# Output squares of a gated delta-rule layer: summed by ScalarE's accumulator, tile by tile, instead of through a buffer and a VectorE sum

## The reference

```
_, out = jax.lax.scan(step, S0, xs)            # the heads' outputs, 128 features each
xn = _rms_norm(out) * norm_w                   # out * rsqrt(mean(out^2) + eps)
gated = jax.nn.silu(z) * xn
return gated.reshape(b_, s_, VALUE_DIM) @ W_out
...
x = _layernorm(x + attention(x));  x = _layernorm(x + experts(x))
```

## Time and profile before

| | |
|---|---|
| median of 3 runs | 1535.07 us (1533.1 to 1536.61) |
| profiled execution | 1533.56 us, its span 1531.8 us |
| PE / PEld busy | 1450.4 us (95%) / 1170.5 us (76%) |
| DVE busy | 1137.3 us (74%) |
| ACT busy | 1067.1 us (70%) |
| POOL busy | 705.5 us (46%) |
| squares L776 | 64 instructions of 128x512, mean 632 ns |
| sums L978 | 64 instructions, mean 677 ns |
| squares of the keys L679 | 128 ACTIVATE of 128x128, mean 293 ns, and 128 accumulator reads, mean 225 ns |

### The profile page before, as it was taken

One profiled execution on the slowest core, in us unless ns is written; L12 is line 12 of the kernel. 1 busy time (PEld: TensorE's weight loads), 2 busy tenths in 40 slices (PEclk: granted clock), 3 DMA queues, 4 the chain that ended last, 5 costly groups with the idle time before them and its releaser, 6 DMA issues.

```text
span 1531.8 us, 38664 instructions
## 1 busy us (share of the span) xinstructions
PE 1450.4 (95%) x14988; PEld 1170.5 (76%) x14988; DVE 1137.3 (74%) x1982; ACT 1067.1 (70%) x2136; POOL 705.5 (46%) x619
## 2 busy tenths in 40 slices
PE   5689999999999999999999999999978899999996
PEld 3468889898888989898888989888864556656565
DVE  5579999999999998999999898999855432312314
ACT  6577878878787787878778777878655365464640
POOL 0544544545454544555454545545316354353540
PEclk9899999999999999999999999999999899999998
DMA  3000202112020311202021120202231112002100
GB/s 113 1 1 23 57 6 53 30 30 36 23 57 2 57 23 36 36 23 56 2 56 20 39 36 23 46 13 43 36 87 51 35 35 69 34 34 69 34 0 28
DMA packets 100985, 55.70 MB, mean 36 GB/s; under 512 B 74572, under 2 KB 93016, under 8 KB 100824
## 3 DMA queue, kind: packets, MB, share of 16 engines
q1 hardware_dynamic: 100824, 53.47, 14.2%
HBM read 35.62 MB, written 1.05 MB: 24 GB/s over the span
## 4 chain that ended last, share of the span: by engine, by line
PE 72%; issue 12%; POOL 8%; DVE 4%; ACT 2%; DMA 1%; POOLq 0%; SPq 0%; DVEq 0%; ACTq 0%
PE bank L387 11%; POOL h L1623 7%; PE bank L542 6%; PE bank L588 5%; PE bank L485 5%; PE bank L529 5%; PE bank L577 4%; PE bank L559 4%; PE bank L568 3%; PE bank L477 3%; PE bank L469 3%; PE bank L1321 3%; PE bank L437 2%; PE bank L438 2%; PE bank L413 2%
## 5 line engine op out<-in xcount | busy, mean ns | idle before, releaser
L874 DVE SCALAR_TENSOR_TENSOR con<-bank,taps,con 128x1022 f32<-128x1022 f32 (+2 forms) x192 | 245.2, 1277 | 13.1 <-ACT con L657 8.6
L1623 POOL TENSOR_TENSOR h<-h 128x512 f16<-128x512 f32 x120 | 148.1, 1242 | 172.4 <-ACT h L1412 166.6
L1516 DVE SCALAR_TENSOR_TENSOR facc<-bank,gcol,facc 128x256 f32<-128x256 f32 x96 | 42.0, 479 | 220.2 <-PE bank L1321 220.2
L1030 POOL TENSOR_TENSOR gl<-const_sb,gc 128x512 f16<-128x512 f32 x128 | 129.7, 1041 | 152.7 <-DVE gc L884 83.0
L387 PE MATMUL bank<-x,qkv 128*128 128x512 f16 x768 | 182.6, 389 | 10.2 <-DVE con L874 10.1
L1305 PE MATMUL bank<-y,w 128*128 128x512 f16 x720 | 166.6, 381 | 8.0 <-ACT h L1412 5.5
L1411 ACT ACTIVATE h<-bank,b 128x512 f32<-128x512 f32 x120 | 82.4, 687 | 127.2 <-PE bank L1305 125.0
L1321 PE MATMUL bank<-w,h 128*128 128x256 f16 x1440 | 160.8, 274 | 0.0
L1321 PEld LDWEIGHTS bank<-w,h 128*128 128x128 f16 x1440 | 141.6, 98 | 19.9 <-issue 0.7
L932 DVE TENSOR_TENSOR X<-X,bank 128x512 f16<-128x512 f16 x192 | 130.0, 683 | 30.7 <-PE bank L477 29.2
L726 ACT ACTIVATE Z<-bank 128x512 f16<-128x512 f16 x192 | 114.2, 606 | 46.2 <-PE bank L485 44.6
(11 more groups left out here) (211 smaller groups left out, 3885.0 us busy)
## 6 DMA issues: line engine op xcount, KB each, us to landing
w<-in_w SPq DMA_DIRECT2D x24, 640.0 KB, 4.5
w_qkv<-in_W_qkvz SPq DMA_DIRECT2D x16, 512.0 KB, 4.1
w_z<-in_W_qkvz SPq DMA_DIRECT2D x16, 256.0 KB, 2.8
w_out<-in_W_out SPq DMA_DIRECT2D x16, 256.0 KB, 3.0
Z<-in_xT SPq DMA_DIRECT2D x2, 512.0 KB, 5.0
y<-in_x SPq DMA_DIRECT2D x1, 1024.0 KB, 8.1
sqo<-oo SPq DMA_TRANSPOSE x64, 3.1
out_dram<-y SPq DMA_DIRECT2D x8, 128.0 KB, 1.8
```

The source lines that it names most:

```text
L874: stt(out=out, in0=bank[:, 0:B, 0:S - k], scalar=taps[:, par, t, TAPS - 1 - k:TAPS - k], in1=out, op0=ALU.mult, op1=ALU.add).then_inc(tap_ ...
L1030: last = tt(gl[:, g % 2, k].rearrange("p (m r) d -> p m r d", m=2), upper.unsqueeze(1).unsqueeze(1).broadcast_to([P, 2, R, P]), gc[:, par, ...
L1623: tt(h16[:, par, 1, t, at], h32[:, k % H32], h16[:, par, 0, t, at], ALU.subtract)\
```

## The change

Squares go to ScalarE's accumulator. For each of the 4 tiles of a chunk, one ACTIVATE (Square, 128x128) with `accum_out` writes the sum of the tile's squares straight to its column of `sso`. The squares themselves are still written, to a place where nobody reads them: the tile's place in the high half of `oo16` (fp16), which "high" overwrites later. The VectorE sums go; its eps step stays and now waits for the fourth square step of its head. `sqo` goes, and `oT` gets memory of its own. The waits change with it: squares now wait for the head before's power (which reads `sso`) and transposes (which read `oo16`), and the transposes of groups 0 and 1 for "op" 2 and 3 of the head before instead of the sums. `sum_done` counts 1 per head instead of 5.

```
+    oT = sb("oT", [P, 2, 2, 4, P], F16)
-    sqo = sb("sqo", [P, 2, B, R, P])
-    oT = sqo[:].rearrange("p s b r d -> p s (b r d)").bitcast(F16).rearrange("p s (k u d) -> p s k u d", k=2, u=4)
...
             sp.wait_ge(oo_low, 4 * n + g + 1)
-            if g < 2:
-                sp.wait_ge(sum_done, 5 * n + 5)
-            else:
-                is_full(sp, n, ("op", g - 2))
+            is_full(sp, n, ("op", g - 2) if g >= 2 else ("op", g + 2, 1))
...
         def square_out(n, par, c):
             is_free(act, n, ("pdl", c))
-            if after(n, 1) or c >= 2:
-                act.wait_ge(sum_done, 5 * n + c - 1)
-            if c < 2:
-                is_full(act, n, ("op", 2 + c, 1))
-            last = do(sqo[:, c % 2], oo[:].rearrange("p (b c r) d -> p b c r d", b=B, c=CH)[:, :, c], ACT.Square)
+            if c == 0 and after(n, 1):
+                act.wait_ge(rso_ready, n + 1)
+            if after(n, 1):
+                act.wait_ge(oT_in[c // 2], 16 * n)
+                act.wait_ge(oT_in[2 + c // 2], 16 * n)
+            for b in range(B):
+                for r in range(R):
+                    u = (b * CH + c) * R + r
+                    last = do(oo16[:, u // 4, 0, u % 4], oo[:, u], ACT.Square, accum_out=sso[:, u:u + 1])
             last.then_inc(sq_out, 1)
...
         def sum_squares(n, par, c):
-            if c == 0 and after(n, 1):
-                dve.wait_ge(rso_ready, n + 1)
-            dve.wait_ge(sq_out, CH * n + c + 1)
-            nc.vector.tensor_reduce(sso[:].rearrange("p (b c r) -> p b c r", b=B, c=CH)[:, :, c], sqo[:, c % 2],
-                                    AX, ALU.add).then_inc(sum_done, 1)
             if c == CH - 1:
-                dve.wait_ge(sum_done, 5 * n + CH)
+                dve.wait_ge(sq_out, CH * n + CH)
...
-            pool.wait_ge(sum_done, 5 * n + 5)
+            pool.wait_ge(sum_done, n + 1)
```

## The result

| | before | changed |
|---|---|---|
| median, lowest to highest | 1535.26 us (1533.1 to 1536.61, 8 runs) | 1539.95 us (1539.13 to 1542.05, 8 runs) |
| profiled execution, span | 1533.56, 1531.8 us | 1539.23, 1537.2 us |
| DVE busy | 1137.3 us | 1100.2 us |
| ACT busy | 1067.1 us | 1103.5 us |

The recorded ratio is 1.0026 with a 95% interval from 1.0017 to 1.0035: slower by 4.0 us (2.6 to 5.4), where the two medians of the table lie 4.7 us apart. The kernel is slower by more than nothing. A second series of the changed kernel gave 1.0027 (1.0015 to 1.0038).

The account below looks back on a forecast made before the run. The prediction took TensorE, idle 0.12 us per head, as full. Waits of 3.15 us plus 0.64 in the last head gave 3.8 us: 1537.4 for the profiled execution, median 1538.9 (+0.25%), range 1534.8 to 1544.

Parts of the forecast that it names:

- The price of a tile: ScalarE's squares: distance between starts of two squared tiles, accumulator read included, 0.29 us; bounds 0.25 and 0.48.
- The row that reads PSUM: Keys' squares, same instruction reading PSUM, 0.25 us per tile; basis of the cheap-tile rival, no new wait, 1535.55, chance 0.30.
- The place: Chunks 2 and 3 on ScalarE: delays add before the "turn" copy, TensorE's L477 waits 0.21 us per head.
- The count of the waits: TensorE's wait behind the "turn" copy, in heads 0 to 14: 15 x 0.21 = 3.15 us.
- Chunks 0 and 1 at nothing: Squares of chunks 0 and 1 on ScalarE: L477 has 0.9 us of slack, cost 0 up to t = 0.40.
- Taps "just in time": VectorE's taps: the copies they need are through at 625.2, and the taps start at 625.24.
- VectorE's relief at nothing: VectorE's four removed sums per head, about 40 us over 16 heads, set nothing earlier for TensorE; costed at 0.
- Last head 0.64: Last head: ScalarE's L1223 behind chunk 3's squares starts 0.64 us later, delaying VectorE's L1233 and L994; cost 0.64 us.
- The signs that the prediction named: Profile after: L477 waits 0.1 to 0.3 us for ACT 15 times, heads last 67.8 us, L1233 waits 0.6 us longer.
- TensorE's reserve: Rival: weight loads busy 58.57 of 67.60 us, so TensorE catches up; only 0.64 us stays, 1535.7, chance 0.08.
- the prices 1562.5 and 1542.6: Times for dearer tiles: 1562.5 at t = 0.48 (dear-tile rival, chance 0.07), 1542.6 at t = 0.32.
- the 1537.4: Forecast for the profiled execution: 3.8 us added to its 1533.56; for a median, 1538.9.

Follow-up runs that it names:

- the kernel without accumulator: Changed kernel with its four narrow squares per chunk but no accumulator output, sums left out; 1537.95 us in one execution.
- the fifth tile: Changed kernel plus a fifth squared tile with accumulator behind chunk 3's four, its result unread; 1544.65 us, ratio 1.0057.
- the sums gone: Kernel before with VectorE's four sums per head left out and nothing in their place, squares 512 columns wide; 1535.97 us, ratio 1.0003.
- the sums put back: Changed kernel with VectorE's four reductions per head back at their old places, over a constant into a spare place; 1541.08 us, ratio 1.0034.
- one exchange in the queue: Changed kernel with ScalarE's turn of level 2, half 1 ahead of chunk 3's squares instead of behind; 1536.46 us, ratio 1.0003.
- the last version above: Changed kernel with the turn ahead of chunk 3's squares and the last head's split of the first experts' weights moved earlier; 1535.64 us, ratio 0.9995.
- the execution that came 4.3 us late to its second head: First execution of the kernel before with the accumulator for chunk 3 alone; 1539.97 us, and 1536.94 us (10 runs) when run again.

## Why the prediction was right

The forecast was 3.8 us more on the profiled execution and a median of 1538.9; the median is 1539.95, the ratio gives 4.0 us (2.6 to 5.4), and the traces give 14 x 0.24 + 0.12 + 0.64 = 4.1 us for the two places that the forecast named.

- The price of a tile: 0.29 forecast, 0.293 measured, in the same two parts, 0.20 and 0.09. The row that reads PSUM, 0.25, would have given no wait. What decided was to take the place that is read from, not only the instruction, from a row.
- The page "ScalarE: Activation LUTs" of the Trainium skill, section "What ACT_TABLE_LOAD costs", has the figures behind the prediction's estimate of 200 ns for 128 columns with an immediate scale; the kernel without accumulator shows 0.20 us. The trace agrees.
- The place: the copy starts at 623.41 of the old time, forecast to the hundredth. That much precision is luck: the table load came 0.03 us earlier than forecast behind the first square, the silu's step was 0.97 instead of 0.94, and two errors of 0.01 cancel as well. The wait was 0.24 instead of 0.21 us: the copy lasted 0.57 instead of 0.59, but from its end to the matmul went 0.10 us instead of the 0.05 taken from the earlier trace rows. Beyond the slack the loss is one to one, as the fifth tile shows.
- The count of the waits: 15 equal ones forecast, 14 and a smaller one found. Head 14 has a next head but no silu to come, so its squares lie otherwise, and it lost 0.12 us. 14 x 0.24 + 0.12 = 3.5 us against the 3.15 of the sum.
- Chunks 0 and 1 at nothing: right, by the kernel that accumulates only those. Taps "just in time": they didn't wait (they start at 625.24 of the old time, as before).
- VectorE's relief at nothing: right in both directions, with the sums gone and with the sums put back. Its busy time fell by 37.1 us, forecast was some 40.
- Last head 0.64: measured 0.64.
- The signs that the prediction named came out but for one: the wait stands under "issue" and not under ScalarE, in heads 0 to 13; a trace read only for waits on ScalarE would have missed it.
- TensorE's reserve: the rival drawn from the page "Perfetto Trace Analysis" of the Trainium skill, section "Identifying the Most-Contended Engine", fell. (The page names MFU beside the weight loads' busy share; the rival used the share alone.) Weight loads were busy for 87% of the head, and still the wait of 0.24 us came out in each head; the fifth tile added its whole length.
- Two of the rivals' prices are not on the footing of the 1537.4: the prices 1562.5 and 1542.6 hold for the median, the sum of the same terms on the profiled execution is 1.5 us less. No verdict hangs on it.
- What the forecast missed is the scatter of the parts outside the heads. The profiled execution of the changed kernel is 5.67 us longer than that of before. 4.35 are there at the last head's weighing, 0.11 of them from the start-up and 0.14 in front of head 14's output product, and 1.0 lies in the output products of the last head. That is the point below. The last 0.3 was not followed.

## What to carry to other kernels

Splitting a wide ScalarE instruction to use the accumulator costs the queue a fixed part for each piece and each read: here a chunk went from 0.52 to 1.17 us, to save 0.64 us on VectorE. Price a moved operation by the row that reads from the same memory, add the delays of all its places in front of the next instruction that the full engine reads, and compare with that one's slack. The engine's idle time alone would have misled here: ScalarE had 13 us of it in a head, and 0.64 us more per chunk still cost. If the sum passes the slack, try the order before the operation: one exchange in the queue gave back all that the heads had lost.

## What was not expected of the hardware

TensorE's clock in the last head. TensorE idles for about 5.7 us ahead of the first output product (6.55 in the last version above), and in the first product the granted clock is 0.50, the level of 1.2 GHz. Windows of the kernel before (first product, then the second):

```profile
1148.80:1151.50 2.70, 2.69 (x13) 1.88 (x14) 0.00 (x0) 0.22 (x1) 1.72 (x3) 0.50 0.23 43
1151.50:1153.20 1.70, 1.57 (x13) 1.08 (x10) 1.57 (x5) 0.00 (x0) 0.00 (x0) 0.89 0.24 49
```

And of the changed kernel:

```profile
1153.15:1155.90 2.75, 2.73 (x14) 1.95 (x15) 0.00 (x0) 0.21 (x1) 1.72 (x3) 0.50 0.23 42
1155.90:1158.50 2.60, 2.55 (x12) 1.51 (x10) 1.88 (x7) 0.00 (x0) 0.46 (x1) 0.50 0.52 101
```

The same 24 matmuls of the first two products took 4.26 us before and 5.28 after: in the second product the granted clock is 0.89 before and still 0.50 after. It isn't the change's doing alone: the kernels with the sums kept, the sums gone and no accumulator took 4.05, 4.14 and 4.07 us, the one with a fifth tile 4.51, the others, among them the one with chunks 0 and 1 only, 5.24 to 5.28. Those that were quick in the first two products, apart from the kernel before and the one with the fifth tile, were slow in the next two (4.4 us for 24), and from the first start to the end of all four they took about 10.5 us, the others 9.9; only the profiled execution of before came through in 8.91 and the fifth tile's in 9.19. What sets it was not settled. For reading it means that a difference of 1 us between two profiled executions can be the clock's at such a place.

A second place like it is the start-up. In the execution that came 4.3 us late to its second head, the second half of x was there for ScalarE at 10.15 us instead of 9.21, which is 0.94 us. In the windows from 20 to 25 and from 25 to 30 us its granted clock was 0.68 and 0.66, against 0.79 and 1.00 in the trace of before. Both differ; how much of the delay each made, and whether the one led to the other, was not settled.
